# Attention scores from two fp32r parts in half arrays instead of three bf16 parts

## The chip, the cores and the metric

The kernel is one launch on one core of a Trainium2 chip. The metric is device time of that launch in microseconds (us), lower is better. The kernel before takes 1335.14 us, the median of three runs (1333.84 to 1339.09).

## The reference

One transformer layer on eight images of 512 tokens, width 256, in float32. The change lies in its attention, which in short is

```
qkv = x @ w_qkv.T + b_qkv                      # x: (8, 512, 256); 16 heads of 16
logits = q @ k.T / sqrt(16)                    # per head, 512 x 512
attn = softmax(logits)
h = (attn @ v, heads side by side) @ w_out.T + b_out
```

A class token is then put in front of the 512 rows, and a linear recurrence over the sequence (a layer norm, a mixing matrix, a scan, another matrix) and a mixture of eight experts with the best two per token follow, each with its residual sum. Those two stages are untouched.

## The kernel before

The program runs four stages one after the other: `stage_qkv`, `stage_attention`, `stage_mix`, `stage_experts`. Every engine has its own instruction list, written out by hand, and semaphores tie them together.

**stage_qkv** (L100 to L291) goes through the eight images. TensorE makes q and k transposed, as four PSUM blocks j of 128 features by 512 tokens (L203, true fp32), and v as four blocks of 128 tokens by 256 (L209). ScalarE adds the bias and copies a block to SBUF (L236). VectorE cuts it into three bf16 parts whose sum is the fp32 value, by a cast, a subtraction, a cast and a subtraction (L263 to L269). SyncE stores the parts (L172, 384 KB per block) and v (L176) in device memory. After the store of image 5, SP loads attention's unit 0 ahead (L185), and then goes on with the stores of images 6 and 7. GpSimd loads x (L150) and at its end writes the ones of the key rows (L155). The stage ends when the last stores have landed.

**stage_attention** (L332 to L638) works on 32 units of four heads of one image (G = 4, `unit(b, g)`, u = 4b + g). `load_unit` (L297) gathers a unit: six products of parts (q0k0, q0k1, q0k2, q1k0, q1k1, q2k0) stand below each other on partitions, 6 x 16 = 96 rows (`KROWS`), so that one bf16 matmul over 96 rows gives fp32-like scores. Scores are made twice:

- `score_by_query` (L469): 128 queries by 512 keys, two units ahead. VectorE takes the negative maximum over keys of two of them at a time (L561). GpSimd cuts the maxima of a unit into three bf16 parts (L381 to L389), TensorE transposes them (L499), ScalarE copies them (L608), and a GpSimd DMA puts them into three further rows of q (L396). With ones in the same rows of k, 99 rows (`SROWS`) give scores minus maximum.
- `score_by_key` (L477): 128 keys by 512 queries, from 99 rows. ScalarE takes the exponential (L613). There are two PSUM buffers, so key matmul j waits for exponential j - 2.

`add_pv` (L489) multiplies the exponentials with v and a column of ones, in fp32, four heads side by side in four column groups of 32. `turn_heads` (L509) transposes the result, and VectorE divides by the sum (L569, L573).

TensorE's order in a unit is fixed: for j = 0 to 15, one key matmul, one query matmul. After j = 4 in between stands the transpose of the maxima, after j = 10 the four transposes of the heads, and after j = 1, 5, 9 and 13 a burst of four pv matmuls (`LATE_PV`, `EARLY_PV`). ScalarE has, beside 16 exponentials, the copy of the maxima after j = 5 and the copy of pv after j = 6. Below, the stretch from the first key matmul after a burst to the first after the next is called a segment; it has four key matmuls a, b, c and d, and the next burst behind d and its query matmul. A unit has four segments.

Of the kernel before, what the change touches and what calls it, by code (L numbers as in the profile page):

```python
# [23 lines left out]
FP32 = mybir.dt.float32  # L24
# [3 lines left out]
ALU = mybir.AluOpType  # L28
# [71 lines left out]
def stage_qkv(nc, mem, dram):  # L100

    wqkv, bqk, bv = mem["wqkv"], mem["bqk"], mem["bv"]
    with ExitStack() as ctx:  # L103
# [3 lines left out]
        qk_full, qk_rest = (mem["wu_e"][:, n:n + 2, :, :].rearrange("p e c n -> p (e c) n") for n in (2, 4))  # L107
        qk_parts = sb("qk_parts", [P, 4, PARTS, S], BF16)
# [19 lines left out]
        cut_step = sem("cut_step")  # L128
# [15 lines left out]
        def _(pool):  # L144
# [8 lines left out]
            pool.memset(mem["max_parts"][:, :, :], 0.0).then_inc(ones_set, 1)  # L153
            pool.wait_ge(ones_set, 2)
            pool.memset(mem["k_rows"][KROWS:SROWS, :, :, :], 1.0)  # L155

        @block.sync
        def _(sp):
# [25 lines left out]
            sp.wait_ge(v_stored, 16)  # L184
            load_unit(sp, mem, dram, 0, 0)  # L185
# [8 lines left out]
        def _(pe):  # L194
            pe.wait_ge(weights_in, 16 * len(mem["first_loads"]))
            with pe.Fori(0, B // 2) as i:
                for par in range(2):
                    b = 2 * i + par
                    pe.wait_ge(x_in[par], 16 * i + 16)
                    for j in range(4):  # L200
                        pe.wait_ge(qk_out[j], b)
# [24 lines left out]
            pe.wait_ge(qk_out[0], B)  # L226
# [19 lines left out]
        def _(dve):  # L246
# [8 lines left out]
            with dve.Fori(0, B // 2) as i:  # L255
                for par in range(2):
                    b = 2 * i + par
                    for j in range(4):
                        full, rest, parts = qk_full[:, j, :], qk_rest[:, j, :], qk_parts[:, j, :, :]
                        n = 12 * b + 3 * j  # L260
# [3 lines left out]
                        dve.wait_ge(cut_step, n + 1)  # L264
                        dve.tensor_tensor(rest, full, parts[:, 0, :], ALU.subtract).then_inc(cut_step, 1)
                        dve.wait_ge(cut_step, n + 2)
                        dve.tensor_copy(parts[:, 1, :], rest).then_inc(cut_step, 1)
                        dve.wait_ge(cut_step, n + 3)
                        dve.tensor_tensor(parts[:, 2, :], rest, parts[:, 1, :], ALU.subtract).then_inc(cut[j], 1)  # L269
# [24 lines left out]
LOADS = 2 * len(Q_PART) + 1  # L294


def load_unit(sp, mem, dram, b, g, v_used=None):  # L297
# [4 lines left out]
    for which, rows, order in ((0, q_rows, Q_PART), (1, k_rows, K_PART)):  # L302
        for n, s in enumerate(order):
            sp.dma_start(rows[HD * n:HD * (n + 1), g, :, :],
                         dram["qk"][bass.ds(b, 1), which, s, G * HD * g:G * HD * (g + 1), :]
                         .rearrange("b (h d) n -> d (b h) n", h=G)).then_inc(done, 16)
# [25 lines left out]
def stage_attention(nc, mem, dram):  # L332

    ident, identb = mem["ident"], mem["identb"]
    with ExitStack() as ctx:
# [6 lines left out]
        max_rows = sb("max_rows", [PARTS * G * TT, P], BF16)  # L342
# [26 lines left out]
        turned_max = turned[:, 0:P // 2].bitcast(BF16)  # L369
# [3 lines left out]
        def _(pool):  # L373
            def split_max(b, g):


                u, rows = NG * b + g, neg_max[:, g % 2, :]
# [3 lines left out]
                pool.tensor_copy(max_parts[:, 0, :], rows).then_inc(max_split, 1)  # L381
                pool.wait_ge(max_split, 4 * u + 1)
                pool.tensor_tensor(neg_rest[:, :], rows, max_parts[:, 0, :], ALU.subtract).then_inc(max_split, 1)
                pool.wait_ge(max_split, 4 * u + 2)
                pool.sem_inc(split_step)
                pool.tensor_copy(max_parts[:, 1, :], neg_rest[:, :]).then_inc(max_split, 1)
                pool.wait_ge(max_split, 4 * u + 3)
                pool.tensor_tensor(max_parts[:, 2, :], neg_rest[:, :], max_parts[:, 1, :],
# [1241 lines left out]
```

## Time and profile before

| what | value |
|---|---|
| median of three runs | 1335.14 us |
| the profiled execution | 1339.97 us, span 1338.2 us |
| PE busy | 1199.1 us (90%), 5606 instructions |
| PE weight loads busy | 695.5 us (52%) |
| DVE busy | 835.4 us (62%) |
| ACT busy | 500.5 us (37%) |
| POOL busy | 405.4 us (30%) |
| DMA moved | 113.04 MB, 84 GB/s over the span |

PE, DVE, ACT, POOL and SP are TensorE, VectorE, ScalarE, GpSimd and SyncE. PEld is the weight load of TensorE, which can lie beside its matmuls. Busy times are sums of records; a matmul's record is longer than the distance to the next one, since matmuls are pipelined. So on PE one reads the starts, not the durations. qkv takes the first 110.9 us, attention the next 448, and the rest belongs to mixing and experts.

### The profile page before, as it was taken

The page shows a single profiled execution, that of the slowest core. Times are in us where ns is not written, and L with a number is a line of the kernel's source. Part 1 is how long each engine was busy: PE and PEld are TensorE (multiplying, and loading weights), DVE is VectorE, ACT ScalarE, POOL GpSimd, SP SyncE. Part 2 cuts the span into 40 slices and gives each one's busy share as a digit, 9 for nine tenths or more (in the row PEclk, how much of TensorE's full clock was granted, in tenths as well). Part 3 has the DMA queues.
Part 4 walks back from the last instruction along what each step waited for, and adds up shares of the span by engine and source line. Part 5 has one row for each costly group of instructions (what it writes and reads, how often), then busy time and mean ns, then how long its engine had stood idle before and what let it go on. Part 6 is the DMA issues. An engine that isn't in the chain of part 4 may idle for free. (4 is left out here: it accounts for less than half of the span.)

```text
span 1338.2 us, 20913 instructions
## 1 busy us (share of the span) xinstructions
PE 1199.1 (90%) x5606; PEld 695.5 (52%) x5607; DVE 835.4 (62%) x1458; ACT 500.5 (37%) x867; POOL 405.4 (30%) x520
## 2 busy tenths in 40 slices
PE   6996999999999999676998899995599999999997
PEld 3651222222222222254665566653488888888885
DVE  4997777777777777156788777776433434333332
ACT  2330777777777777521111222213212222121211
POOL 1021431111111111012332344335444545454543
PEclk9995999999999999887999999998799999999999
DMA  8895223232323222005311444310133333333232
GB/s 280 302 282 166 65 86 91 87 87 88 102 73 101 89 85 64 17 16 126 95 47 49 94 94 94 78 33 17 25 53 50 51 52 48 54 47 55 47 50 37
DMA packets 108674, 113.04 MB, mean 84 GB/s; under 512 B 26080, under 2 KB 97904, under 8 KB 107600
## 3 DMA queue, kind: packets, MB, share of 16 engines
q1 hardware_dynamic: 90528, 89.05, 23.4%
q0 software_dynamic: 18112, 23.57, 10.1%
q8 instruction: 17, 0.28, 0.1%
q14 instruction: 17, 0.14, 0.0%
HBM read 68.81 MB, written 43.62 MB: 84 GB/s over the span
## 5 line engine op out<-in xcount | busy, mean ns | idle before, releaser
L561 DVE TENSOR_REDUCE neg_max<-by_query 128x2 f32<-128x1024 f32 x256 | 308.2, 1223 | 100.4 <-PE by_query L469 98.8
L613 ACT ACTIVATE k_wu_e<-by_key 128x512 f32<-128x512 f32 x512 | 285.4, 597 | 130.5 <-PE by_key L477 129.1
L477 PE MATMUL by_key<-k_wg_e 99*128 99x512 bf16 x512 | 197.8, 388 | 22.1 <-ACT k_wu_e L613 14.9
L469 PE MATMUL by_query<-k_wg_e 96*128 96x512 bf16 x512 | 200.4, 399 | 11.2 <-PEq L103 7.5
L477 PEld LDWEIGHTS by_key<-k_wg_e 99*128 99x128 bf16 x512 | 49.1, 97 | 231.7 <-issue 113.0
L1324 POOL DMA_INDIRECT out_rows<-y,slot x72 | 113.2, 1573 | 182.0 <-DVE y L1461 176.6
L1417 ACT ACTIVATE gate<-ps_up 128x512 f32<-128x512 f32 x72 | 43.2, 600 | 303.9 <-PE ps_up L69 303.9
L489 PE MATMUL pv<-k_wu_e,k_wd_e 128*32 128x512 f32 x1024 | 136.2, 604 | 1.1 <-ACT k_wu_e L613 1.1
L1377 PE MATMUL ps_y<-k_wd_e,acts_T 128*128 x576 | 136.1, 379 | 0.8 <-ACT acts_T L1426 0.8
L1377 PEld LDWEIGHTS ps_y<-k_wd_e,acts_T 128*128 128x128 f32 x576 | 109.1, 190 | 18.6 <-issue 1.0
L1445 DVE CAST x_T<-ps_x 128x256 fp32r<-128x256 f32 x72 | 30.6, 424 | 107.2 <-PE ps_x L1351 107.2
L381 POOL CAST k_max_parts<-neg_max 128x16 bf16<-128x16 f32 x32 | 6.2, 193 | 281.9 <-DVE neg_max L561 281.9
L1461 DVE TENSOR_SCALAR y<-ps_y,slot 128x256 f32<-128x256 f32 x72 | 34.8, 483 | 78.0 <-DMA out_rows<-y,slot 54.7
L1314 POOL DMA_INDIRECT x_in<-kept_x_rows,slot x72 | 73.8, 1024 | 31.1 <-issue 21.6
L1454 DVE TENSOR_TENSOR acts<-gate,ps_up 128x512 f32<-128x512 f32 x72 | 49.5, 687 | 52.3 <-PE ps_up L69 52.3
L69 PE MATMUL ps_up<-wg_short,x_T 128*128 x144 | 70.9, 492 | 5.3 <-issue 5.3
L469 PEld LDWEIGHTS by_query<-k_wg_e 96*128 96x128 bf16 x512 | 49.7, 100 | 42.2 <-DVE neg_max L561 13.2
L817 POOL DMA_INDIRECT kept_table<-k_pay,k_slot_i x64 | 63.9, 999 | 24.4 <-issue 18.4
L790 POOL TENSOR_TENSOR mix_rstd<-mix_mv,k_minus_half 128x4 f32<-128x4 f32 x16 | 16.4, 1028 | 179.5 <-DVE mix_mv L1078 177.4
L203 PE MATMUL qk_ps<-k_wu_e,k_wqkv 128*128 128x512 f32 x128 | 59.3, 618 | 12.1 <-DMA k_wu_e<-in_xT 12.1
L928 PE MATMUL mix_pairs<-mix_u_T,k_wg_s 128*128 128x512 f32 x128 | 63.3, 618 | 1.1 <-DVE mix_act_T L1056 1.1
L69 PE MATMUL ps_up<-wu_short,x_T 128*128 x144 | 63.2, 439 | 0.0
(211 smaller groups left out, 1900.6 us busy)
## 6 DMA issues: line engine op xcount, KB each, us to landing
k_wg_e<-kept_qk SPq DMA_DIRECT2D x384, 64.0 KB, 2.2
kept_qk<-qk_parts SPq DMA_DIRECT2D x32, 384.0 KB, 3.4
kept_v<-v_ones SPq DMA_DIRECT2D x8, 1024.0 KB, 5.8
k_wd_e<-kept_v SPq DMA_DIRECT2D x32, 256.0 KB, 3.1
k_wu_e<-in_xT POOLq DMA_DIRECT2D x8, 512.0 KB, 4.5
kept_heads<-k_wd_e SPq DMA_DIRECT2D x8, 512.0 KB, 3.0
k_heads_in<-kept_heads SPq DMA_DIRECT2D x8, 512.0 KB, 4.0
k_wg_e<-in_wg_e SPq DMA_DIRECT2D x8, 512.0 KB
```

Of the source, the lines that this page charges most:

```text
L69: mm = pe.matmul(out, short(lhs[a]), short(rhs[b]), start=(start and n == 0), stop=(stop and n == 2))
L203: mm = pe.matmul(qk_ps[:, j, :], wqkv[:, c, j * P:(j + 1) * P], xt[:, par, c, :], start=(c == 0), stop=(c == DC - 1))
L469: pe.matmul(by_query[:, k % 4, :], q_rows[0:KROWS, g, h, t * P:(t + 1) * P], k_rows[0:KROWS, g, h, :], start=True, stop=True).then_inc(que ...
L477: pe.matmul(by_key[:, j % 2, :], k_rows[0:SROWS, g, h, kt * P:(kt + 1) * P], q_rows[0:SROWS, g, h, :], start=True, stop=True).then_inc(key ...
L489: mm = pe.matmul(pv[VW * h:VW * (h + 1), :], v_unit[:, g, kt, h, :], probs[:, G * (kt // 2) + h, kt % 2, :], start=(kt == 0), stop=(kt == ...
L561: dve.tensor_reduce(neg_max[:, g % 2, 2 * n:2 * n + 2], by_query[:, 2 * (n % 2):2 * (n % 2) + 2, :], AX.X, ALU.max, negate=True).then_inc( ...
L613: act.activation(probs[:, key_tile(j) // 2 * G + j // 2 % G, j % 2, :], by_key[:, j % 2, :], ACT.Exp, scale=float(HD) ** -0.5).then_inc(ex ...
L817: pool.indirect_dma_start(out=dram["table"], in_offset=None, in_=mem["pay"][:, t, n, :], out_offset=bass.IndirectOffsetOnAxis(ap=mem["slot ...
L928: mm = pe.matmul(pairs[:, m % 2, n, :], w[:, c, m * P:(m + 1) * P], u2_T[:, c, :], start=(c == 0), stop=(c == DC - 1))
L1314: pool.indirect_dma_start(out=x_in[:, r % X, :], out_offset=None, in_=dram["x_rows"], in_offset=bass.IndirectOffsetOnAxis(ap=slot[:, r % R ...
L1324: pool.indirect_dma_start(out=dram["out"], in_=y[:, r % 2, :], in_offset=None, compute_op=ALU.add, out_offset=bass.IndirectOffsetOnAxis(ap ...
L1377: mm = pe.matmul(ps_y[:, r % 2, 0:D], acts_T[:, m, :], mem["wd_e"][:, bass.ds(e, 1), m, :], start=(m == 0), stop=(m == FC - 1))
```

## The change

q and k are cut into two parts in fp32r (the fp32 format that a matmul takes in one pass), three products (q0k0, q0k1, q1k0), so 48 rows per head and 50 with the two rows of the maxima. Heads go in pairs: the even head's rows are at partitions 0 to 49, the odd head's at 64 to 113. Key matmul j takes half j % 2, the query matmul beside it the other half. ScalarE writes the first part straight from PSUM and VectorE the second in one instruction, (PSUM + bias) - first part. In the cut maxima there are two parts as well, transposed in fp32. The ones of the keys are now a fill of the whole key tensor, and the load of unit 0 waits for it. A unit is still gathered with 12 DMAs of 64 KB; the store of a block is 512 KB.

```diff
-PARTS = 3
-Q_PART = (0, 0, 0, 1, 1, 2)
-K_PART = (0, 1, 2, 0, 1, 0)
+PARTS = 2
+Q_PART = (0, 0, 1)
+K_PART = (0, 1, 0)
+HALF = P // 2
+HP = G // 2
...
-            pool.memset(mem["max_parts"][:, :, :], 0.0).then_inc(ones_set, 1)
+            pool.memset(mem["max_parts"][:, :], 0.0).then_inc(ones_set, 1)
             pool.wait_ge(ones_set, 2)
-            pool.memset(mem["k_rows"][KROWS:SROWS, :, :, :], 1.0)
+            pool.memset(mem["k_rows"][:, :, :, :], 1.0).then_inc(ones_set, 1)
...
+            sp.wait_ge(ones_set, 3)
             load_unit(sp, mem, dram, 0, 0)
...
-                        pe.wait_ge(qk_out[j], b)
+                        pe.wait_ge(cut[j], b)
...
-                    act.wait_ge(cut[j], b)
+                    act.wait_ge(parts_stored[j], 16 * b)
                     act.wait_ge(qk_made, 4 * b + j + 1)
-                    act.activation(qk_full[:, j, :], qk_ps[:, j, :], ACT.Identity,
+                    act.activation(short(qk_parts[:, j, 0, :]), qk_ps[:, j, :], ACT.Identity,
...
-                        dve.wait_ge(parts_stored[j], 16 * b)
                         dve.wait_ge(qk_out[j], b + 1)
-                        dve.tensor_copy(parts[:, 0, :], full).then_inc(cut_step, 1)
...
-                        dve.tensor_tensor(parts[:, 2, :], rest, parts[:, 1, :], ALU.subtract).then_inc(cut[j], 1)
+                        dve.scalar_tensor_tensor(short(parts[:, 1, :]), qk_ps[:, j, :], bqk[:, j:j + 1], parts[:, 0, :],
+                                                 ALU.add, ALU.subtract).then_inc(cut[j], 1)
...
-            sp.dma_start(rows[HD * n:HD * (n + 1), g, :, :],
...
+            for hh in range(2):
+                first = HALF * hh + HD * n
+                sp.dma_start(rows[first:first + HD, g, :, :], heads[hh]).then_inc(done, 16)
...
-                pool.dma_start(q_rows[KROWS:SROWS, g, :, :].rearrange("s h (t p) -> s (h t) p", t=TT),
-                               max_rows[:, :]).then_inc(max_in[g], 16)
+                for hh in range(2):
+                    first = HALF * hh + KROWS
+                    pool.dma_start(q_rows[first:first + PARTS, g, :, :].rearrange("s h (t p) -> s (h t) p", t=TT),
+                                   max_rows[PARTS * HP * TT * hh:PARTS * HP * TT * (hh + 1), :]).then_inc(max_in[g], 16)
...
+        def key_step(j):
+
+            return j // 4, j // 2 % HP, j % 2
+
+        def query_step(k):
+
+
+            return k // (2 * TT), k // 2 % TT, 1 - k % 2
...
+                hp, t, hh = query_step(k)
+                rows = slice(HALF * hh, HALF * hh + KROWS)
...
                 pe.matmul(by_query[:, k % 4, :],
-                          q_rows[0:KROWS, g, h, t * P:(t + 1) * P], k_rows[0:KROWS, g, h, :],
+                          short(q_rows[rows, g, hp, t * P:(t + 1) * P]), short(k_rows[rows, g, hp, :]),
...
+                kt, hp, hh = key_step(j)
+                rows = slice(HALF * hh, HALF * hh + SROWS)
...
-                pe.matmul(by_key[:, j % 2, :], k_rows[0:SROWS, g, h, kt * P:(kt + 1) * P],
-                          q_rows[0:SROWS, g, h, :], start=True, stop=True).then_inc(key_scored, 1)
+                pe.matmul(by_key[:, j % 2, :], short(k_rows[rows, g, hp, kt * P:(kt + 1) * P]),
+                          short(q_rows[rows, g, hp, :]), start=True, stop=True).then_inc(key_scored, 1)
...
-                if kt % 2 == 0:
-                    for buf in range(2):
-                        pe.wait_ge(exp_done[buf], G * TT // 2 * u + G + 2 * kt)
+                for buf in range(2):
+                    pe.wait_ge(exp_done[buf], G * TT // 2 * u + G // 2 * (kt + 1))
...
-                pe.transpose(turned_max, max_parts[:, :, :].rearrange("p s n -> p (s n)"),
-                             identb[:, :]).then_inc(max_turned, 1)
+                pe.transpose(turned_max, max_parts[:, :], ident[:, :]).then_inc(max_turned, 1)
```

How this moves instructions shows at two places. The first is VectorE's list in the qkv stage, one image of eight; `k_wu_e` is the SBUF place of the full and the rest values, `qk_ps` the PSUM block. The difference:

```order
-L263 CAST qk_parts<-k_wu_e 128x512
-L264 REGISTER_ALU
-L265 TENSOR_TENSOR k_wu_e<-k_wu_e,qk_parts 128x512
-L266 REGISTER_ALU
-L267 CAST qk_parts<-k_wu_e 128x512
-L268 REGISTER_ALU
-L269 TENSOR_TENSOR qk_parts<-k_wu_e,qk_parts 128x512
...
+L262 SCALAR_TENSOR_TENSOR qk_parts<-qk_ps,k_bqk,qk_parts 128x512 x4
```

The four instructions per block, with a wait between each, are gone, and one per block stands in their place, four in a row for an image.

The second is SyncE's list at the end of the qkv stage, where unit 0 is loaded between the stores; before:

```order
L304 DMA k_wg_e<-kept_qk 16x4x512 [waits parts_stored3,parts_stored2,v_stored,parts_stored1,parts_stored0]
L304 DMA k_wg_e<-kept_qk 16x4x512 x11
L309 DMA k_wd_e<-kept_v 128x4x128
L172 DMA kept_qk<-qk_parts 128x3x512 [waits cut0]
L172 DMA kept_qk<-qk_parts 128x3x512 [waits cut1]
```

and of the change:

```order
L302 DMA q_rows<-kept_qk 16x2x512 [waits parts_stored3,v_stored,parts_stored2,ones_set,parts_stored1,parts_stored0]
L302 DMA q_rows<-kept_qk 16x2x512 x5
L302 DMA k_rows<-kept_qk 16x2x512 x6
L305 DMA k_wd_e<-kept_v 128x4x128
L172 DMA kept_qk<-qk_parts 128x2x512 [waits cut0]
L172 DMA kept_qk<-qk_parts 128x2x512 [waits cut1]
```

The count of DMAs is the same, 13. The first one has a further wait, for the fill of the key tensor by GpSimd, and the stores of image 6 stand behind it. TensorE's order of instructions in a unit is the same before and after: key, query, transposes and bursts keep their places.

## Rows read from the trace of the kernel before

**Rows 1.** By stretch: length; PE, PEld, DVE, ACT, POOL busy; clock, DMA share, GB/s.
```profile
40.00:60.00 20.00, 20.00 (x64) 11.89 (x63) 19.22 (x40) 7.51 (x10) 1.45 (x2) 1.00 0.85 306
...
110.00:132.00 22.00, 16.27 (x33) 2.57 (x33) 18.63 (x16) 0.27 (x1) 5.34 (x25) 0.50 0.49 133
132.00:559.00 427.00, 404.18 (x2171) 114.95 (x2171) 305.55 (x303) 302.28 (x575) 64.77 (x231) 0.99 0.27 81
```

**Rows 2.** Groups of instructions, 200 to 500 us: count, busy us, mean ns, idle time before.
```profile
L561 DVE TENSOR_REDUCE neg_max<-by_query 128x2 f32<-128x1024 f32 x181 | 218.1, 1223 | 70.7 <-PE by_query L469 69.6
L613 ACT ACTIVATE k_wu_e<-by_key 128x512 f32<-128x512 f32 x360 | 200.7, 597 | 87.2 <-PE by_key L477 86.4
```

**Rows 3.** Timeline of PE and ACT, one whole segment: start us, us, engine, instruction.
```profile
303.73 0.39 PE L477 MATMUL by_key<-k_wg_e 99*128 99x512 bf16 x1
303.96 0.38 PE L469 MATMUL by_query<-k_wg_e 96*128 96x512 bf16 x1
304.16 2.16 ACT L613 ACTIVATE k_wu_e<-by_key 128x512 f32<-128x512 f32 x4 [0.94 <-PE by_key L477]
...
305.30 0.39 PE L477 MATMUL by_key<-k_wg_e 99*128 99x512 bf16 x1
305.53 0.38 PE L469 MATMUL by_query<-k_wg_e 96*128 96x512 bf16 x1
305.84 1.07 PE L489 MATMUL pv<-k_wu_e,k_wd_e 128*32 128x512 f32 x8
306.83 0.39 PE L477 MATMUL by_key<-k_wg_e 99*128 99x512 bf16 x1
```

**Rows 4.** Timeline of PE in unit 30, which has no query matmuls.
```profile
542.53 0.60 PE L477 MATMUL by_key<-k_wg_e 99*128 99x512 bf16 x2
...
545.42 0.60 PE L477 MATMUL by_key<-k_wg_e 99*128 99x512 bf16 x2
```

**Rows 5.** Timeline of PEld and PE: a bf16 load after a wait; fp32r loads, experts.
```profile
305.30 0.10 PEld L477 LDWEIGHTS by_key<-k_wg_e 99*128 99x128 bf16 x1 [0.30 <-ACT k_wu_e L613]
...
1150.72 0.19 PEld L69 LDWEIGHTS ps_up<-wu_short,x_T 128*128 128x128 f32 x1
1150.83 0.19 PEld L69 LDWEIGHTS ps_up<-wu_rest,x_T 128*128 128x128 f32 x1
...
1150.75 0.48 PE L69 MATMUL ps_up<-wu_short,x_T 128*128 x1
1151.07 0.39 PE L69 MATMUL ps_up<-wu_rest,x_T 128*128 x1
1151.30 0.39 PE L69 MATMUL ps_up<-wu_short,x_rest 128*128 x1
```

**Rows 6.** Timeline of PE: transposes of heads in two units, and of the maxima.
```profile
300.69 0.60 PE L509 MATMUL turned<-k_ident,heads_T 128*128 128x128 f32 x4
...
308.14 0.22 PE L499 MATMUL turned<-k_identb,k_max_parts 128*128 128x128 bf16 x1
...
314.01 0.60 PE L509 MATMUL turned<-k_ident,heads_T 128*128 128x128 f32 x4
```

**Rows 7.** Timeline of all engines, start of the program and end of qkv.
```profile
0.84 1.80 POOL L145 MEMSET v_ones<- 128x2048 f32 x1 [0.29 <-POOLq L1618]
...
78.94 6.92 POOL L155 MEMSET k_wg_e<- 3x8192 bf16 x1
79.76 6.38 DVE L263 CAST qk_parts<-k_wu_e 128x512 bf16<-128x512 f32 x1
...
80.71 3.34 SPq L304 DMA_DIRECT2D k_wg_e<-kept_qk  x4
...
87.41 7.03 PE L203 MATMUL qk_ps<-k_wu_e,k_wqkv 128*128 128x512 f32 x16
...
106.48 0.35 SPq L176 DMA_DIRECT2D kept_v<-v_ones  x1
...
110.93 6.84 SPq L304 DMA_DIRECT2D k_wg_e<-kept_qk  x12
```

More of the change, by code:

```diff
@@ L106, in stage_qkv @@
         xt = mem["wu_e"][:, 0:2, :, :]
-        qk_full, qk_rest = (mem["wu_e"][:, n:n + 2, :, :].rearrange("p e c n -> p (e c) n") for n in (2, 4))
-        qk_parts = sb("qk_parts", [P, 4, PARTS, S], BF16)
+        qk_parts = sb("qk_parts", [P, 4, PARTS, S], FP32)
         v_ones = sb("v_ones", [P, TT, H, VW], FP32)
@@ L258, in _ @@
                     for j in range(4):
-                        full, rest, parts = qk_full[:, j, :], qk_rest[:, j, :], qk_parts[:, j, :, :]
-                        n = 12 * b + 3 * j
-                        dve.wait_ge(parts_stored[j], 16 * b)
+                        parts = qk_parts[:, j, :, :]
                         dve.wait_ge(qk_out[j], b + 1)
-                        dve.tensor_copy(parts[:, 0, :], full).then_inc(cut_step, 1)
[L264 to L268, printed above, removed]
-                        dve.tensor_tensor(parts[:, 2, :], rest, parts[:, 1, :], ALU.subtract).then_inc(cut[j], 1)
+                        dve.scalar_tensor_tensor(short(parts[:, 1, :]), qk_ps[:, j, :], bqk[:, j:j + 1], parts[:, 0, :],
+                                                 ALU.add, ALU.subtract).then_inc(cut[j], 1)
                     dve.wait_ge(v_stored, 16 * b)
@@ L303, in load_unit @@
         for n, s in enumerate(order):
-            sp.dma_start(rows[HD * n:HD * (n + 1), g, :, :],
-                         dram["qk"][bass.ds(b, 1), which, s, G * HD * g:G * HD * (g + 1), :]
-                         .rearrange("b (h d) n -> d (b h) n", h=G)).then_inc(done, 16)
+            heads = (dram["qk"][bass.ds(b, 1), which, s, G * HD * g:G * HD * (g + 1), :]
+                     .rearrange("b (hp hh d) n -> hh d (b hp) n", hp=HP, hh=2))
+            for hh in range(2):
+                first = HALF * hh + HD * n
+                sp.dma_start(rows[first:first + HD, g, :, :], heads[hh]).then_inc(done, 16)
     if v_used is not None:
@@ L368, in stage_attention @@
         block = ctx.enter_context(nc.Block())
-        turned_max = turned[:, 0:P // 2].bitcast(BF16)
+        turned_max = turned[:, 0:P]
+        by_half = max_parts[:, 0:PARTS * G * TT].rearrange("p (hh s hp t) -> p hh s hp t", hh=2, s=PARTS, hp=HP)
+        max_short, max_rest = (by_half[:, :, s, :, :].rearrange("p hh hp t -> p hp t hh") for s in range(PARTS))
         LAST = B - 1
@@ L374, in split_max @@
             def split_max(b, g):
-                u, rows = NG * b + g, neg_max[:, g % 2, :]
+                u = NG * b + g
+                rows = neg_max[:, g % 2, :].rearrange("p (hp t hh) -> p hp t hh", hp=HP, t=TT)
                 pool.wait_ge(max_taken, G * TT // 2 * (u + 1))
@@ L380, in split_max @@
                 pool.sem_inc(split_step)
[L381 to L388, printed above, removed]
-                                   ALU.subtract).then_inc(max_split, 1)
+                pool.tensor_copy(short(max_short), rows).then_inc(max_split, 1)
+                pool.wait_ge(max_split, 2 * u + 1)
+                pool.tensor_tensor(short(max_rest), rows, max_short, ALU.subtract).then_inc(max_split, 1)
             def place_max(b, g):
@@ L1576, in program @@
                 mem[name] = later.enter_context(nc.sbuf_tensor(name, [P, E, DC, F], FP32))
+        with ExitStack() as early:
+            for name in ("q_rows", "k_rows"):
+                mem[name] = early.enter_context(nc.sbuf_tensor(name, [P, NG, HP, S], FP32))
         until_cut = ctx.enter_context(ExitStack())
```

33 lines of the change are left out of this document (13 added, 20 removed).

## The prediction

> **What bounds the kernel now.** I read the views from coarse to fine: busy time by stretch, groups of instructions, then the timeline.
>
> By stretch [rows 1], qkv has PE busy 20.00 of 20.00 us and DVE 19.22, DMA at a share of 0.85. In attention from 132 us on PE has 404 of 427 us, DVE 306, ACT 302, at a granted clock of 0.99. So PE looks like the bound of both. But a PE record is longer than PE's work, so the groups count: ACT's exponential group sat idle 87.2 us in 300, waiting for key matmuls, and DVE's reduction 70.7 us, waiting for query matmuls [rows 2]. PE is late for both. Why it is late shows one segment [rows 3], 3.10 us from key matmul a (303.73) to a of the next (306.83):
>
> - a to its exponential: 0.43 (303.73 to 304.16);
> - two exponentials (2.16 less 0.60 is 1.56 for three, so 0.52 to 0.54 apart; the last lasts 0.60): 1.14, until key matmul d may start (305.30);
> - d, then its query matmul 0.23 later, and 0.31 after that the pv burst (305.84): 0.54;
> - the burst, 0.99.
>
> So the path is a latency ring, burst, a, exponentials a and b, d, query d, burst. Of the query matmuls only the one behind d lies on it. The others fill time in which PE waits anyway. Unit 30, without query matmuls, confirms it: its segment takes 2.89 us (542.53 to 545.42) [rows 4], just 0.21 less, though four matmuls of 0.22 are gone. A unit takes 13.32 us (300.69 to 314.01 between turns of heads) [rows 6]. By the busy times of the stretch, DVE needs 306/427 of that, 9.5 us, and ACT 9.4 us [rows 1], so neither becomes the bound soon.
>
> **Attention, part by part.** The change acts on the ring in four ways.
>
> *The halves.* Query d no longer waits for the array, since its rows lie in the other half. No row shows two half-array matmuls at once; the nearest is the pv burst, where eight fp32 records in four column groups take 0.99 us [rows 3], while sixteen fp32 records of the same 512 columns over the whole array take 7.03, 0.44 each [rows 7], so eight in turn would take 3.5. So parts of the array do work at once here. Bound: 0.22 saved per segment (all of query d), or nothing (the halves take turns). If the two weight loads go one after the other, a load's 0.11 (1150.72 to 1150.83 [rows 5]) remains of it. I take 0.17, between a free and a serial load.
>
> The Trainium skill, TensorE: Matmul & The Clock Gate, Part 3, says that matmuls in different row groups run concurrently with starts about 4 ns apart. By it the saving would be the whole 0.22 and the sum 6 us lower. No row here shows it.
>
> *The loads.* A bf16 load after a wait is invisible: d waits for ACT, its load [rows 5] and its matmul [rows 3] both start at 305.30, and the next matmul follows at 0.23. An fp32r load is visible: the first fp32r matmul after transposes has its follower 0.32 later (1150.75 to 1151.07), the next 0.23 (1151.30) [rows 5]. So 0.09 per exposed load, and it is exposed wherever PE comes out of a burst or of a wait: at a and at d, 0.18 per segment. Bounds: 0 and 2 x 0.19, the record's whole length. fp32r matmuls follow at 0.23 against 0.22 for bf16; with two at once that is 0.01.
>
> So a plain segment changes by 0.18 + 0.01 - 0.17, about +0.02, four times 0.08.
>
> *The transposes.* They use all rows of the array between half-array matmuls, so their own load and that of the matmul behind no longer hide: about 0.09 each. Those of the heads delay key matmul b and through it d: +0.18 less 0.11, the part of query a that now overlaps, is 0.07. That of the maxima grows from 0.08 (308.14 [rows 6] to its query) to 0.11 and stands before d: with one load 0.12, of which little slack hides anything. Together I take +0.17, between 0 and 0.5.
>
> *The waits of pv and the maxima's DMAs.* The bursts' waits are met long before. The two GpSimd DMAs instead of one delay the maxima's rows by one issue, some 0.6 us; they are needed only a few us later at the next unit's first key matmul. Nothing, and if the cover is gone, 0.6 a unit. SyncE's 13 DMAs per unit carry the same bytes: nothing.
>
> Sum per unit +0.25 us (from -0.9, all loads hidden and query d free, to +1.5, halves in turn and every load exposed). Times 30 units: +7.5 us. The last two units lose nothing and pay 8 loads of 0.09 each: +1.4. At the end, the third pv burst no longer waits for the last exponential: -0.9. Attention: **+8.0 us**.
>
> **The qkv stage.** PE sets the pace there and keeps its matmuls. DVE's four instructions per block become one, so its backlog goes, and with it the cast that took 6.38 us while GpSimd's fill ran for 6.92 [rows 7]. What that is worth is read at the end: the last image's q and k matmuls begin at 87.41, and the image's v would be done 10.3 us later, at 97.7; I allow DVE 1 us for the last v, then SyncE would issue its store at 98.8 instead of 106.48, and attention starts 4.45 later, as before (106.48 to 110.93). That would be -7.7. Against it stands the new wait. SyncE starts unit 0's loads at 80.71 now; after the change when the fill ends, 4096 columns at 1.80 us per 2048 [rows 7], 3.6 from 78.94, so 82.6, 1.9 us later. The stores of image 6 are queued behind these 13 DMAs, and ScalarE's part of image 7 now waits for them, since it writes into the stored tile itself. Stores are also a third larger, with the DMA share at 0.85 [rows 1]. I take half of this delay to show: **-5.5 us**, between -7.7 and 0 (DMA becomes the bound). Attention's first 22 us are DVE's reductions (18.63 of 22 us [rows 1]) and loads: unchanged.
>
> **The sum**: +8.0 - 5.5 = +2.5 us. The profiled execution took 1339.97 us, 4.8 above the median of 1335.14; I set the difference against the median: 1337.6, so **1338 us**, own range 1329 to 1347.
>
> **The rivals.**
>
> *Loads hide, halves overlap* (faster). If a half's load lies under the other half's work or the burst, all of the 0.22 goes and 0.09s don't come: -0.88 per unit, +0.2 for the transposes, say -0.6: -18, with qkv -5.5 and the end -0.9: 1311. For it: two halves are separate resources. Against it: the load stands behind the wait on PE, as at 305.30 [rows 5].
>
> *The halves take turns* (slower). fp32r matmuls in half arrays run one after another, or share a path. Then query d costs its 0.23 as before, and the loads come on top: 0.19 to 0.2 per segment, 0.15 more for the transposes, +0.95 per unit, +28.5; with +1.4, -0.9 and -5.5: 1359. It decides as soon as the followers of a key matmul come 0.2 us later. For it: no row shows half-array overlap. Against it: the burst.
>
> *Switching costs* (slower or equal). From scores to burst the gap is 0.31 instead of 0.22 [rows 3], so 0.09 goes into the change of the array's division. The change adds four such changes per unit, around the two transposes: +0.36 per unit, +11: 1349. Against it: not all lie on the ring. The Trainium skill, TensorEngine Tiling (Array Packing), Key Properties, says that changing the tiling mode drains the engine; the 0.31 agrees, and whether half-array and full-array are two modes in its sense no run here shows.
>
> *The change does nothing* (equal): ring 3.10 as before, and qkv PE-bound to the end; it is inside the first forecast's range.
>
> **How the numbers follow.** Under 0.5% (6.7 us) a measurement of this kernel can't tell from no change. Forecast 0.42, loads hide 0.24, switching 0.18, turns 0.13, other slower 0.03. Faster: 0.24 and a seventh of the forecast, 0.30. Same: 0.7 of the forecast and a sixth of the switching, 0.33. Slower: the rest, 0.37. The range for 8 in 10 reaches from the first rival, 1311, to 1362, just past the turns; the halves of the two outer cases beyond it are the 2 in 10 left out.
>
> **What would show it.** In the changed profile: qkv's DVE near half busy, attention's first load at 104 to 107 us instead of 110.93. Segments of 3.1 us, units of 13.4 to 13.8. Query matmuls starting 0.0 to 0.11 us after their key matmul (0.23 would be the turns). a to its exponential 0.52 instead of 0.43; if it stays at 0.43, the loads hide. The gap around the transposes shows the switching. Wrong would be the whole frame if ACT or DVE had no idle time left, if the granted clock fell below 1 in attention, or if the maxima's DMAs released the first key matmul of a unit.

## The result, and the profile after

The changed kernel takes **1358.93 us** (median of 4 runs, 1355.53 to 1365.53) against 1334.49 (4 runs, 1331.83 to 1339.09): ratio 1.0185, 95% interval [1.0137, 1.0234]. It is slower by 1.9%. The forecast was 1338, the range 1311 to 1362.

The profiled execution took 1365.53 us, span 1363.8 (before 1339.97 and 1338.2). The 25.6 us between the two are found by stretch, from the times at which PE turns the heads of a unit (the transposes at L509 before, L508 after):

| stretch | before | after | difference |
|---|---|---|---|
| start to attention's first query matmul | 110.97 | 106.61 | -4.4 |
| from there to the heads of the third unit | 69.7 | 86.5 | +16.8 |
| 26 units | 346.60 | 359.60 | +13.0 |
| last three intervals between heads | 31.7 | 44.4 | +12.7 |
| from there to the experts' first x transpose | 382.8 | 372.1 | -10.7 |
| experts | 396.4 | 394.6 | -1.8 |

Attention is 42.5 us longer, not the 8 of the forecast. The last two lines hold code that the change leaves alone. In the twelve profiles (the two above and those of the ten experiments below) the last line but one is 372 to 378 us in the six kernels made from the change and 377 to 387 in the six bf16 ones. It tends to be shorter with the change, then, and scatters by 10 us within one kind; why, I did not find.

The stretches show where the two large terms come from. First of the kernel before (the columns are those of [rows 1]):

```profile
140.00:160.00 20.00, 19.24 (x109) 4.91 (x101) 15.51 (x15) 13.91 (x27) 6.50 (x28) 1.00 0.21 61
...
540.00:560.00 20.00, 15.10 (x88) 3.83 (x86) 1.62 (x5) 13.13 (x24) 0.00 (x0) 1.00 0.00 0
```

and of the changed kernel:

```profile
40.00:60.00 20.00, 20.00 (x64) 11.84 (x63) 8.56 (x16) 8.06 (x10) 1.45 (x2) 1.00 0.99 359
...
140.00:160.00 20.00, 18.95 (x69) 5.93 (x67) 8.83 (x8) 8.86 (x18) 5.90 (x24) 0.50 0.20 55
160.00:180.00 20.00, 18.69 (x69) 5.84 (x67) 10.03 (x10) 9.26 (x18) 7.46 (x24) 0.51 0.20 53
180.00:560.00 380.00, 317.79 (x1893) 117.08 (x1893) 279.51 (x275) 262.01 (x494) 48.87 (x126) 1.00 0.30 84
560.00:580.00 20.00, 16.47 (x59) 5.26 (x63) 0.68 (x2) 11.22 (x22) 1.14 (x2) 0.64 0.01 2
580.00:600.00 20.00, 15.49 (x58) 4.10 (x50) 1.87 (x7) 6.70 (x13) 0.00 (x0) 0.59 0.03 12
```

Read the clock column against the count of matmuls. From 140 to 160 us the kernel before is at 1.00 (2.4 GHz) and makes 109 matmuls; the changed one is at 0.50 (1.2 GHz) and makes 69, and as many in the 20 us behind. PE's busy share, 19 of 20 us, is the same in both, since a record is longer at half clock (a key matmul's 0.79 us instead of 0.50) and the next one starts before it ends: this column hides the loss. The clock comes back at about 180. It falls again in the last two units, where no query matmuls are left; before, the same two units kept 1.00 with PE busy for only 15.10 us of 20. In qkv the DMA share has gone from 0.85 [rows 1] to 0.99, and DVE from 19.22 us to 8.56.

The groups of instructions from 200 to 500 us, at full clock, beside [rows 2]:

```profile
L560 DVE TENSOR_REDUCE neg_max<-by_query 128x2 f32<-128x1024 f32 x173 | 209.7, 1222 | 78.5 <-PE by_query L470 78.1
L613 ACT ACTIVATE k_wu_e<-by_key 128x512 f32<-128x512 f32 x348 | 196.4, 598 | 93.3 <-PE by_key L479 86.1
```

An exponential and a reduction cost what they did (598 and 1222 ns). Both engines idle longer, for the same releaser: PE is still what they wait for. In 300 us there are 348 exponentials instead of 360, which is the unit of 13.83 us instead of 13.32.

Where a unit's 0.51 us arise is shown by its timeline, PE and ACT, columns as in [rows 3]. First the plain segment:

```profile
306.99 0.50 PE L479 MATMUL by_key<-q_rows,k_rows 50*128 50x512 f32 x1
306.99 0.73 PE L470 MATMUL by_query<-k_rows,q_rows 48*128 48x512 f32 x2
...
307.52 2.27 ACT L613 ACTIVATE k_wu_e<-by_key 128x512 f32<-128x512 f32 x4 [0.83 <-PE by_key L479]
...
308.66 0.18 PEld L479 LDWEIGHTS by_key<-q_rows,k_rows 50*128 50x128 f32 x1 [0.21 <-ACT k_wu_e L613]
308.66 0.50 PE L479 MATMUL by_key<-q_rows,k_rows 50*128 50x512 f32 x1
308.66 0.18 PEld L470 LDWEIGHTS by_query<-k_rows,q_rows 48*128 48x128 f32 x1
308.67 0.50 PE L470 MATMUL by_query<-k_rows,q_rows 48*128 48x512 f32 x1
...
309.10 1.06 PE L490 MATMUL pv<-k_wu_e,k_wd_e 128*32 128x512 f32 x8
310.09 0.50 PE L479 MATMUL by_key<-q_rows,k_rows 50*128 50x512 f32 x1
```

Key matmul d and query matmul d start together (308.66, 308.67), and so do their loads (308.66). From d to the burst it is 0.44 us instead of 0.54, from key a to its exponential 0.53 instead of 0.43, and the segment takes 306.99 to 310.09, 3.10 us as before [rows 3]. Then the two segments with transposes:

```profile
303.36 0.50 PE L479 MATMUL by_key<-q_rows,k_rows 50*128 50x512 f32 x1
303.37 0.50 PE L470 MATMUL by_query<-k_rows,q_rows 48*128 48x512 f32 x1
303.80 0.66 PE L508 MATMUL turned<-k_ident,heads_T 128*128 128x128 f32 x4
304.38 0.50 PE L479 MATMUL by_key<-q_rows,k_rows 50*128 50x512 f32 x1
...
311.27 0.49 PE L479 MATMUL by_key<-q_rows,k_rows 50*128 50x512 f32 x1 [0.45 <-ACT k_wu_e L613]
311.70 0.33 PE L499 MATMUL turned<-k_ident,k_max_parts 128*128 128x128 f32 x1
...
312.62 1.07 PE L490 MATMUL pv<-k_wu_e,k_wd_e 128*32 128x512 f32 x8
313.61 0.50 PE L479 MATMUL by_key<-q_rows,k_rows 50*128 50x512 f32 x1
```

The segment of the heads, 303.36 to 306.99, takes 3.63 us, 0.14 more than before; that of the maxima, 310.09 to 313.61, 3.52 instead of 3.15 (306.83 to 309.98). The fourth stays at 3.58 to 3.59. So the whole +0.51 is that of the two segments with transposes. Key c at 311.27 to the burst at 312.62 takes 1.35 us; in the plain segment 308.17 to 309.10, 0.93.

### The profile page after: what moved, and what is told of

Read it like the earlier page. It is cut to its first block and busy times, and to the rows that moved or that the text cites. A ratio compares the mean times of both kernels' runs of the same rounds, so it can differ in the third digit from the quotient of the medians.

```text
span 1363.8 us, 20724 instructions
## 1 busy us (share of the span) xinstructions
PE 1184.8 (87%) x5606; PEld 723.5 (53%) x5607; DVE 788.4 (58%) x1362; ACT 503.4 (37%) x867; POOL 405.9 (30%) x488
## 5 line engine op out<-in xcount | busy, mean ns | idle before, releaser
L560 DVE TENSOR_REDUCE neg_max<-by_query 128x2 f32<-128x1024 f32 x256 | 309.2, 1222 | 130.6 <-PE by_query L470 129.4
L613 ACT ACTIVATE k_wu_e<-by_key 128x512 f32<-128x512 f32 x512 | 288.7, 597 | 170.7 <-PE by_key L479 161.6
L479 PE MATMUL by_key<-q_rows,k_rows 50*128 50x512 f32 x512 | 227.5, 498 | 72.7 <-ACT k_wu_e L613 70.6
L479 PEld LDWEIGHTS by_key<-q_rows,k_rows 50*128 50x128 f32 x512 | 91.7, 198 | 268.5 <-ACT k_wu_e L613 146.0
L470 PE MATMUL by_query<-k_rows,q_rows 48*128 48x512 f32 x512 | 209.2, 512 | 12.5 <-PEq L105 6.2
L490 PE MATMUL pv<-k_wu_e,k_wd_e 128*32 128x512 f32 x1024 | 150.4, 663 | 0.0
L470 PEld LDWEIGHTS by_query<-k_rows,q_rows 48*128 48x128 f32 x512 | 84.2, 200 | 23.0 <-DVE neg_max L560 11.3
L380 POOL CAST k_max_parts<-neg_max 128x16 fp32r<-128x16 f32 x32 | 6.8, 212 | 277.8 <-DVE neg_max L560 277.8
L391 POOL DMA_DIRECT2D q_rows<-max_rows x64 | 36.7, 575 | 120.6 <-ACT max_rows L607 113.6
```

Of the source, the lines that this page charges most:

```text
L470: pe.matmul(by_query[:, k % 4, :], short(q_rows[rows, g, hp, t * P:(t + 1) * P]), short(k_rows[rows, g, hp, :]), start=True, stop=True).th ...
L479: pe.matmul(by_key[:, j % 2, :], short(k_rows[rows, g, hp, kt * P:(kt + 1) * P]), short(q_rows[rows, g, hp, :]), start=True, stop=True).th ...
L490: mm = pe.matmul(pv[VW * h:VW * (h + 1), :], v_unit[:, g, kt, h, :], probs[:, 2 * kt + h // 2, h % 2, :], start=(kt == 0), stop=(kt == TT ...
L560: dve.tensor_reduce(neg_max[:, g % 2, 2 * n:2 * n + 2], by_query[:, 2 * (n % 2):2 * (n % 2) + 2, :], AX.X, ALU.max, negate=True).then_inc( ...
L613: act.activation(probs[:, 2 * kt + hp, hh, :], by_key[:, j % 2, :], ACT.Exp, scale=float(HD) ** -0.5).then_inc(exp_done[j % 2], 1)
```

## The experiments

I held two theories on the clock. A: it follows how busy PE is, and PE with overlapping halves has more idle time. B: it follows how much of the array works at once, and a half-array matmul by itself counts less. Each time below goes with a before timed beside it, of which the ratio is made: 1332.34 us (7 runs) for the first four experiments; 1333.63 (7) for bf16 over half the rows and for query c ahead as well; 1336.9 (13) for the other four.

**Both matmuls in the same half.** The query takes the key's half, so it can't overlap with its key matmul:

```
-            return k // (2 * TT), k // 2 % TT, 1 - k % 2
+            return k // (2 * TT), k // 2 % TT, k % 2
```

> The change, but each query matmul takes the same half of the array as the key matmul before it, so the two cannot overlap. Theory A (what the overlap is worth, and the clock goes with how busy TensorE is): query matmul d is back on the ring, 0.23 us per segment, so a steady unit goes from 13.83 to about 14.7 us (+26 us); TensorE has fewer gaps at the start of attention, so the granted clock is back at 1.0 some 15 to 30 us earlier than in the change (-8 to -12 us); the last two units have no queries and stay at half clock. Total near 1375. Rival B (the clock stays low because only half of the array's rows are used): start as cold as in the change, total near 1385. Rival C (the halves never overlapped usefully): unit stays at 13.83.

1621.4 us, ratio 1.2165 [1.2138, 1.2192]. A window of 40 us late in attention:

```profile
740.00:780.00 40.00, 38.13 (x124) 12.90 (x122) 18.14 (x18) 16.93 (x32) 2.71 (x6) 0.50 0.17 49
```

PE has records for 95% of the time, and the clock stays at 0.50 through all of attention, with units of 22.75 us; both totals that I expected (1375, 1385) were far too low. The change itself ran at 1.00 with 317.79 of 380 us, 84%. So the share of recorded busy time does not decide the clock, and A falls.

What differs is that a key matmul and its query matmul stand one behind the other in one half. The halves are not kept apart altogether, though. The next key matmul lies in the other half, and where it waits for nothing the two start together, as a and b of a segment do here, and their queries behind them:

```profile
744.90 0.80 PE L479 MATMUL by_key<-q_rows,k_rows 50*128 50x512 f32 x2
```

So this run shows that the clock did not come back with this order. It does not show what one half working alone does, nor whether the kernel would have kept a full clock once it had one.

**The maxima's transpose later.** `turn_max` goes from after key matmul 4 of a unit to after 6, into the segment in which PE waits longest for ACT anyway, and ACT's copy of the result behind exponential 7:

```
-                    if j == 4 and next_max:
+                    if j == 6 and next_max:
                         turn_max(b1, g1)
```

> The change, but the transpose of the maxima stands after key matmul j = 6 instead of j = 4 (where ScalarE is busy with the copy of pv and key matmul b has slack), and ScalarE's copy of the maxima after exponential 7. Theory A (the +0.37 us of the segment with this transpose is the drain of the halves before a full-array transpose and its exposed load, standing before key matmul d on the ring): the segment falls from 3.52 to about 3.10 and nothing else grows, unit 13.83 to about 13.45, total 11 us less than the change, near 1348. Rival (the cost is PE work that moves along): the segment with the copy of pv grows by as much, unit 13.8, no change.

1353.94 us, ratio 1.0155 [1.0111, 1.0199]. A unit takes 13.41 us, 0.42 less. PE around the moved transpose:

```profile
368.92 0.50 PE L479 MATMUL by_key<-q_rows,k_rows 50*128 50x512 f32 x1
...
372.03 0.50 PE L479 MATMUL by_key<-q_rows,k_rows 50*128 50x512 f32 x1
372.46 0.33 PE L499 MATMUL turned<-k_ident,k_max_parts 128*128 128x128 f32 x1
...
374.19 0.50 PE L479 MATMUL by_key<-q_rows,k_rows 50*128 50x512 f32 x1 [0.41 <-ACT k_wu_e L613]
```

The segment that held it is plain now (3.11 us), and the one that holds it takes the 3.59 it took without it: key d there still waits 0.41 us for ACT, so the transpose and its changes are covered. That shows the transposes' share of a unit. By the total alone the gain is not clear of noise (the two intervals overlap), and at the medians it is less than the 11 us that 27 units of 0.42 give. The profiled execution stayed at half clock until 206 us (0.50 in every window of 20 us from 120 to 200), later than the change's; the start took 91.9 us instead of 86.5, the last three intervals 39.3 instead of 44.4.

**More half-array work where the clock was low.** In the first two units every query matmul is made twice, and in the last two an idle one into the free half stands behind each key matmul, 64 in all (of the edit only the calls are shown; `more_work` makes a query matmul whose result nobody reads):

```
                     if ahead:
+                        if isinstance(b, int) and b == 0 and g < 2:
+                            more_work(b2, g2, j)
                         score_by_query(b2, g2, j)
+                    else:
+                        more_work(b, g, j)
```

> The change, with 64 further half-array matmuls whose results nobody reads: each query matmul of units 0 and 1 is made twice, and in the last two units, which have no queries, an idle query matmul stands behind each key matmul. Theory A (the half clock at both ends of attention, 16.8 us lost at the start and 12.7 at the end, comes from TensorE being too little busy): the granted clock of the last two units is 1.0, they take about 27.5 us instead of 44 from the heads of unit 28 on, and the start warms earlier: 10 to 22 us less than the change, 1337 to 1349. Rival B (half-array matmuls do not hold the clock, however many): the clock stays at 0.6 there and the time is equal or up to 5 us longer.

1351.14 us, ratio 1.0142 [1.0122, 1.0162]. Two of its windows, early in attention and in the last units:

```profile
140.00:160.00 20.00, 18.48 (x117) 7.42 (x117) 13.97 (x13) 13.09 (x26) 5.90 (x24) 1.00 0.20 57
...
560.00:580.00 20.00, 14.03 (x92) 4.57 (x88) 2.19 (x8) 10.97 (x20) 0.19 (x1) 1.00 0.06 26
```

With 64 useless matmuls the kernel is 7.8 us faster than the change at the medians (the intervals of the ratios still touch), less than the 10 to 22 that I expected. The last three intervals fall from 44.4 to 34.7 us, and the clock stays at 1.00 in them with PE busy 14.03 of 20 us, less than the 16.47 and 15.49 of the change's two windows there. The start falls from 86.5 to 75.0 us; units between stay at 13.83. So idle work takes back 9.7 of the 12.7 us at the end and, in this execution, 11.5 of the 16.8 at the start.

**The same type over all rows.** Both matmuls take rows 0 to 113 (key) and 0 to 111 (query), so that they sum the scores of two heads, and the fill of the query tensor with zeros is added at the start (shown is the key matmul's edit):

```
-                rows = slice(HALF * hh, HALF * hh + SROWS)
+                rows = slice(0, HALF + SROWS)
```

> The change with matmuls over all rows: key and query scores take rows 0 to 113 at once, so what is computed is the sum of two heads' scores (one thing left out: the heads are not told apart), in fp32r, with no halves. GpSimd fills the query tensor too (3.5 us more before unit 0 is loaded). It takes the halves away and keeps the fp32r loads. Theory A (loads exposed by 0.11 at key matmuls a and d, no drain around the transposes): unit 13.32 + 8 x 0.10 = about 14.1 to 14.2, the transpose of the maxima cheap again (segment 3.3 instead of 3.52), and the clock back as early as in the kernel before because TensorE has more to do. Total 1350 to 1362. Rival (loads cost nothing and all of the +0.5 is the halves): unit 13.3 to 13.4.

1365.52 us, ratio 1.0241 [1.0226, 1.0255]. The same two windows:

```profile
140.00:160.00 20.00, 19.60 (x98) 8.76 (x99) 14.09 (x15) 12.93 (x25) 6.31 (x25) 1.00 0.21 55
...
560.00:580.00 20.00, 17.36 (x88) 6.08 (x87) 3.87 (x7) 14.30 (x27) 1.58 (x4) 1.00 0.01 2
```

The clock is back by 140 us and does not fall in the last two units, with nothing added. A unit takes 14.37 us, more than the 14.1 to 14.2 that I expected, and one plain segment (359.89 to 363.22 in PE's timeline) 3.33:

```profile
356.14 0.50 PE L481 MATMUL by_key<-q_rows,k_rows 114*128 114x512 f32 x1
356.48 0.39 PE L472 MATMUL by_query<-k_rows,q_rows 112*128 112x512 f32 x1
356.71 0.60 PE L510 MATMUL turned<-k_ident,heads_T 128*128 128x128 f32 x4
357.06 0.48 PE L481 MATMUL by_key<-q_rows,k_rows 114*128 114x512 f32 x1
...
359.89 0.50 PE L481 MATMUL by_key<-q_rows,k_rows 114*128 114x512 f32 x1
...
363.22 0.50 PE L481 MATMUL by_key<-q_rows,k_rows 114*128 114x512 f32 x1
```

So fp32r over all rows, with the change's other edits, costs 14.37 - 13.32 = 1.05 us a unit, and the halves give 0.54 of it back. A load that stands behind a wait costs 0.11: key to query is 0.34 here (356.14 to 356.48) and 0.23 where the load hides. And without a change of the array's division the query is followed by the transposes after 0.23 us and those by the key after 0.35; in halves these are 0.43 (303.37 to 303.80) and 0.58 (303.80 to 304.38).

**bf16 over half the rows.** In the kernel before, the score matmuls take only rows 0 to 63, which leaves out part of the products and the maxima (the query matmul is edited likewise):

```
-                pe.matmul(by_key[:, j % 2, :], k_rows[0:SROWS, g, h, kt * P:(kt + 1) * P],
-                          q_rows[0:SROWS, g, h, :], start=True, stop=True).then_inc(key_scored, 1)
+                pe.matmul(by_key[:, j % 2, :], k_rows[0:P // 2, g, h, kt * P:(kt + 1) * P],
+                          q_rows[0:P // 2, g, h, :], start=True, stop=True).then_inc(key_scored, 1)
```

> The kernel before, in bf16, with its score matmuls over rows 0 to 63 only (left out: two of the six products, and the maxima, so the exponentials are of scores without their maximum). The instructions, their columns, order and waits stay. Theory A (the half clock of the variant with both matmuls in one half comes from matmuls that use half of the rows, whatever their type): the granted clock stays at 0.5 through attention, units of 20 us or more, total above 1530. Rival B (it came from fp32r in half arrays, or from something else in that variant): clock 1.0, unit 13.3, time as the kernel before.

1386.12 us, one run. By stretch:

```profile
160.00:240.00 80.00, 79.92 (x254) 18.04 (x254) 37.75 (x38) 36.62 (x66) 15.98 (x52) 0.53 0.17 51
240.00:560.00 320.00, 306.34 (x1615) 80.38 (x1608) 238.04 (x233) 221.41 (x421) 34.11 (x120) 1.00 0.29 87
```

With PE recorded busy for 79.92 of 80 us the clock is at 0.53; it comes back at 235 us, some 100 us later than with 96 to 99 rows of the same type (before 140, above). My expectation that it stays low throughout was wrong. For the late return at the start fp32r is not needed, then: half of the array is enough. But these matmuls all lie in the same half, with none beside them, and from 235 us on they kept 1.00, in the last two units too, with PE busy 16.20 of 20 us:

```profile
580.00:600.00 20.00, 16.20 (x90) 3.69 (x82) 3.31 (x5) 14.75 (x29) 1.44 (x5) 1.00 0.01 2
```

There the change fell to half clock. So half-array matmuls alone don't explain the loss at the end; fp32r, or 50 rows instead of 64, has a part in it, and no run separates those two. This run also separates the second cost; PE's timeline around the transposes of the heads:

```profile
316.25 0.38 PE L469 MATMUL by_query<-k_wg_e 64*128 64x512 bf16 x1
316.55 0.66 PE L509 MATMUL turned<-k_ident,heads_T 128*128 128x128 f32 x4
317.14 0.39 PE L477 MATMUL by_key<-k_wg_e 64*128 64x512 bf16 x1
```

At full clock the plain segment is 3.11 us as before, while query to transposes takes 0.30 instead of 0.22 and transposes to key 0.59 instead of 0.44. A unit takes 13.71 to 13.73 us, 0.39 more, with not one fp32r matmul in it. What the segments with transposes take above a plain one:

| kernel | heads | maxima |
|---|---|---|
| before, bf16, 96 to 99 rows | 0.39 | 0.05 |
| fp32r, 112 to 114 rows | 0.42 | 0.10 |
| bf16, 64 rows | 0.62 | 0.19 |
| the change, fp32r in halves | 0.53 | 0.42 |

**Transpose moved and work added together** (the edits of the two runs above, on the change):

> The change with both repairs: transpose of the maxima after j = 6, and the 64 idle or repeated query matmuls in the first and the last two units. Theory A (the two costs are separate and add): unit 13.40, granted clock 1.0 from 145 us to the end of attention, 13 us less than with the idle matmuls alone (1351), near 1338, so still no better than the kernel before. Rival (shorter units leave the array emptier, the clock falls at the ends again): 1345 or more.

1347.73 us (10 runs), ratio 1.0074 [1.005, 1.0097]: the best of the half-array versions, still slower than before, and in the rival's range, not near 1338. Units take 13.40 us as expected, and the end is at full clock. But the start was not: the clock was 0.50 from 140 to 160 us and 0.66 from 160 to 180, with the same added work with which it was at 1.00 from 140 us on in the other run. So what idle work does at the start is not shown by either.

**The gain without halves.** If only query d stands on the ring, it can go ahead of the key matmul that waits for ACT, in bf16:

```
                 for j in range(G * TT):
+                    if ahead and j % 4 == 1:
+                        score_by_query(b2, g2, j)
                     score_by_key(b, g, j)
...
-                    if ahead:
+                    if ahead and j % 4 != 1:
```

> The kernel before (three bf16 parts, all of the array), with one change: in each segment query matmul d is issued before key matmul d, in the time in which TensorE waits for exponential b. Theory A (query d on the ring is all that the halves could win, and the order wins it without them): the three segments without the transpose of the maxima lose 0.22 us each, in the one with it TensorE is busy up to d, so nothing; unit 13.32 to 12.66, 30 units, 20 us less than the kernel before, near 1313. Rival (VectorE or the waits for its maxima hold query d, or TensorE's own work is the bound): unit stays above 13.2 and the time at 1330 or more.

1320.2 us where 1313 was expected, ratio 0.9881 [0.9843, 0.992]. A unit takes 12.88 us (mean of 26): 0.45 less, not the 0.66 that I expected. PE's timeline in its plain segment (321.80 to 324.92) shows why:

```profile
322.97 0.38 PE L477 MATMUL by_key<-k_wg_e 99*128 99x512 bf16 x1
323.18 0.59 PE L469 MATMUL by_query<-k_wg_e 96*128 96x512 bf16 x2
323.62 0.38 PE L477 MATMUL by_key<-k_wg_e 99*128 99x512 bf16 x1
```

Queries c and d now stand together between key c and key d, and d comes 0.65 us after c, when ACT has long been done. There the wait was too short to hold two.

**With the transpose moved too** (the same edit as on the change):

> As the one with the query first, and the transpose of the maxima after key matmul j = 6, ScalarE's copy of them after exponential 7. Theory A: the fourth segment loses 0.22 us too, unit 12.44, 26 us less than the kernel before, near 1307. Rival: DVE (9.5 us of work per unit) or the later maxima (their rows must be in place before the next unit's first key matmul) hold the unit at 12.7 or more.

1322.16 us, ratio 0.987 [0.9832, 0.9909]; a unit takes 12.79 us (mean of 26), not the 12.44 expected. The transpose of the maxima costs next to nothing in this kernel, 0.05, so there was little to win, and in the total nothing shows.

**And the fill taken away from GpSimd.** VectorE writes the key tensor's rows of ones at the program's start:

```
-            pool.wait_ge(ones_set, 2)
-            pool.memset(mem["k_rows"][KROWS:SROWS, :, :, :], 1.0)
...
             dve.memset(mem["minus_half"][:, :], -0.5)
+            dve.memset(mem["k_rows"][KROWS:SROWS, :, :, :], 1.0)
```

> As the one before, and the ones of the key rows are written by VectorE at the very start, where it waits for weights, instead of by GpSimd beside VectorE's casts at the end of the qkv stage. Theory A: the cast of 6.38 us becomes 0.42, VectorE ends the stage some 5 us earlier, attention starts at 106 to 107 instead of 110.93: 3 to 5 us less, near 1303. That would be all that the change wins in qkv, without its two parts. Rival (the stores' DMAs set that end): same time as without.

**1315.81 us**, ratio 0.9838 [0.9785, 0.9892]: the fastest median here, though not the 1303 expected. Attention begins at 107.77 us instead of 110.61 in the version before this one; that part, 2.8 us, of the qkv gain had nothing to do with fp32r.

**Query c ahead as well** (the condition `j % 4 == 1` becomes `j % 4 < 2`):

> As the one with the fill moved to VectorE, and query matmul c too stands before its key matmul, in the 0.4 us in which TensorE waits for exponential a. Theory A (in the last one the plain segments stayed at 3.13 because both queries, c and d, then stood between key c and key d, 0.22 us too much): the plain segments fall to 2.9, unit 12.83 to 12.4, 12 us less, near 1304. Rival (VectorE's reductions, 9.9 us and their waits, hold the queries, and a query ahead of a key then delays that key): unit 12.8 or more, no gain or a loss.

1316.16 us, ratio 0.9864 [0.9846, 0.9883]; units of 12.79 to 12.88, no gain, as the rival has it. PE's timeline over two segments:

```profile
318.96 0.39 PE L468 MATMUL by_query<-k_wg_e 96*128 96x512 bf16 x1 [0.23 <-DVE neg_max L562]
...
320.94 0.39 PE L476 MATMUL by_key<-k_wg_e 99*128 99x512 bf16 x1
...
323.82 0.39 PE L476 MATMUL by_key<-k_wg_e 99*128 99x512 bf16 x1
```

One segment falls to 2.88 us (320.94 to 323.82), close to the 2.89 without queries [rows 4], but the next to it takes 3.25: query c waits for a free buffer from VectorE, and key c waits behind it. A matmul is to be put ahead of a wait only if it waits for nothing itself.

## Why the prediction was right or wrong

**What bounds attention: right.** The ring decides. The plain segment was forecast at +0.02 and came out at 3.10, unchanged, from two terms that cancel as described.

**The halves: right, sized too low.** The forecast took 0.17 between 0.22 and 0.11. The starts lie 0.00 to 0.01 us apart, the two loads start together too, and d to burst falls by 0.10, which is the 0.22 less a load of 0.11. So the whole 0.22 is saved. The Trainium skill, TensorE: Matmul & The Clock Gate, Part 3, says that matmuls in different row groups run concurrently; this trace agrees.

**The loads: right.** 0.09 at a and at d were forecast, 0.10 to 0.11 measured. a to its exponential was to be 0.52 and is 0.53 to 0.54. The rival in which loads hide is dead: over all rows, where nothing is won back, a plain segment takes 3.33 us instead of 3.10, two loads of 0.11.

**The transposes: wrong by three times.** The forecast took +0.17 a unit; it is 0.14 + 0.37 = 0.51. The step that failed was to price them by the exposed loads alone, 0.09 each. The bound of 0.5 was the value. The rival on switching named the mechanism and gave +0.36; the run with bf16 over 64 rows shows it without fp32r, and the run over all rows shows fp32r without it. In the sum it makes 30 times 0.34, 10 us.

**The granted clock: no term at all.** I noted the 0.50 of the first 22 us of attention [rows 1] and wrote "unchanged", and named a clock below 1 only among the things that would break the frame. The two stretches with half clock became 16.8 and 12.7 us longer, where +1.4 was forecast: the largest part of the error. The question not asked was what a matmul over half the rows does to a clock that the kernel before had to win back in attention too.

What the runs show of the cause differs between the two ends:

- Neither the share of PE's record time decides (95% busy at 0.50, 75% at 1.00) nor fp32r by itself: over all rows the clock was back at 137 us and did not fall in the last units.
- At the start the clock was back at 131 to 138 us in the six profiled executions with score matmuls over 96 rows or more. With 64 rows or fewer it was back at 140, 174, 180, 206 and 235 us, and in one not before the end of attention. bf16 over 64 rows is among them, so the type is not needed.
- At the end two runs with idle work in the free half kept 1.00, so the missing partner matters there. But bf16 over 64 rows kept 1.00 too, without a partner.

So that the clock was lost with the half-array layout is shown. By which of its properties, rows, type or how the halves alternate, is not.

**qkv: right in kind, close in size.** -5.5 forecast, -4.4 measured, at 106.6 us where 104 to 107 was said. The end of the stage after the change:

```profile
81.46 2.78 SPq L302 DMA_DIRECT2D q_rows<-kept_qk  x6
...
91.66 1.28 ACT L237 ACT_TABLE_LOAD   x1 [7.91 <-DMA kept_qk<-qk_parts]
...
99.86 0.35 SPq L176 DMA_DIRECT2D kept_v<-v_ones  x1
...
106.57 2.50 SPq L302 DMA_DIRECT2D q_rows<-kept_qk  x3
```

Unit 0's first load is issued at 81.46, right behind the fill, where 82.6 was forecast. The last v's store is issued at 99.86, near the 98.8 forecast, instead of 106.48 [rows 7]. ScalarE waits 7.91 us for image 6's stores, the new wait that was named. The last step, store to load, takes 6.71 us where I had kept 4.45; the DMA share of 1.04 from 90 to 100 us (0.88 before) makes a queue likely, but no run tested it.

**The last pv burst and the maxima's second DMA.** No row contradicts their terms (-0.9 and 0), but the fall of the clock covers the former.

**The total.** By the prediction's own parts: qkv -4.4, attention +42.5, which on the median of 1335.14 would have been 1373, outside the range. The stages that the change leaves alone took 12.5 us less in this pair of executions and brought the time back into it; that was luck. 1358.93 stands on the 1359 of the rival in which halves take turns, and that rival is false. It had the number by accident, and the wide range held for a reason that it did not contain. Of the three outcomes slower had the highest chance, 0.37, but of its mechanisms the one that was real, switching, was priced at 11 us, a part of the loss.

**Open.** When the clock comes back at the start is not settled: the two versions with the same added work, one profiled execution each, had it back at 140 and 174 us, so part of the 16.8 us can be scatter between executions. Nor is it settled why the mixing stage after attention scatters between 372 and 387 us, and whether its being shorter in kernels with the change belongs to it. Not tried was a version of the change whose first units use all rows and the later ones the halves.

## What to carry to other kernels

A matmul on a latency ring can be taken off it by order alone: put it into the wait ahead of the instruction that waits, provided it is ready itself. Here that gave 1.2% with three lines, while the new layout cost 1.9%. Before rows are halved to let two matmuls run side by side, look at where PE is at 1.2 GHz and at where one of the two partners is missing: there the clock can be lost, and the busy column does not show it. Full-array transposes between half-array matmuls belong where the engine waits anyway.

## What the runs showed of the hardware

- The granted clock is not explained by how long PE has records. It stayed at 0.53 with 79.92 of 80 us busy (bf16 over 64 rows) and at 0.50 with 95% (fp32r, the query behind its key in one half), and at 1.00 with 70% (14.03 of 20 us) where both halves had work, with 75% (15.10 of 20) over 99 rows and with 81% (16.20 of 20) over 64 rows in bf16.
- The load of one half does not wait for that of the other: both start within 0.01 us (308.66).
- An fp32r matmul of 512 columns follows at 0.23 to 0.24 us, a bf16 one at 0.22, but behind a wait fp32r's load is visible, 0.10 to 0.11 us, in full rows and in halves alike.
- Going from half-array to full-array matmuls and back costs about 0.23 us at four transposes in bf16 (0.08 before, 0.15 behind), 0.43 in fp32r (0.20 and 0.23, against the run over all rows).
